# A two-layer graph kernel on one core: Gelu in place in the accumulators, the residual added from PSUM in one instruction, and the next sweep opened behind that add

## What is computed

```python
x = x + gnn0(relu(layernorm(x)), adj)   # max over the first 25 neighbours, concat, W0, bias, relu
h = relu(layernorm(x)) @ W              # layer 1: attention over the graph
e   = leaky_relu(s1[:, :, None] + s2[:, None, :], 0.4)   # s1 = h @ a1, s2 = h @ a2
att = softmax(where(adj > 0, e, -1e20), axis=1)
x = x + gelu(att @ h)
# 8 graphs (batches), N = 2048 nodes, C = 256 channels, fp32
```

## Time and profile before

| what | value |
|---|---|
| time, median of 3 runs | 4289.71 us (4282.42 to 4291.24) |
| the profiled execution: its own time | 4286.7 us |
| its span, first to last instruction | 4284.9 us |
| POOL busy | 3099.6 us (72%), 3205 instructions |
| DVE busy | 3347.2 us (78%) |
| PE busy | 2678.6 us (63%) |
| ACT busy | 1963.2 us (46%) |
| mean granted TensorE clock | 0.716 of full speed |

### The profile page before, as it was taken

One profiled execution on the slowest core, in us unless ns is written; L12 is line 12 of the kernel. 1 busy time (PEld: TensorE's weight loads), 2 busy tenths in 40 slices (PEclk: granted clock), 3 DMA queues, 4 the chain that ended last, 5 costly groups with the idle time before them and its releaser, 6 DMA issues. The chain is left out here.

```text
span 4284.9 us, 43700 instructions
## 1 busy us (share of the span) xinstructions
PE 2678.6 (63%) x13568; PEld 1997.2 (47%) x13568; DVE 3347.2 (78%) x7261; ACT 1963.2 (46%) x2364; POOL 3099.6 (72%) x3205
## 2 busy tenths in 40 slices
PE   2334446666666676566666666666666666666669
PEld 2222235444454554455444544455445445545457
DVE  5666689966898669986799768996689866998655
ACT  4222255632665236643466325553256532664146
POOL 5777777777777777777777777777777777777720
PEclk8555556777777777777777777777777767777779
DMA  6555556666666766666666666667666666666531
GB/s 211 169 158 181 175 183 215 209 221 217 204 214 208 232 214 196 216 219 227 202 217 204 224 214 214 216 198 230 209 213 219 206 220 225 193 214 203 175 109 55
DMA packets 412751, 860.10 MB, mean 201 GB/s; under 512 B 67299, under 2 KB 248422, under 8 KB 396134
## 3 DMA queue, kind: packets, MB, share of 16 engines
q0 software_dynamic: 153600, 419.64, 31.8%
q1 hardware_dynamic: 258918, 437.67, 30.2%
HBM read 714.43 MB, written 142.61 MB: 200 GB/s over the span
## 5 line engine op out<-in xcount | busy, mean ns | idle before, releaser
L411 POOL DMA_INDIRECT gb<-h_table,idx x3200 | 3098.9, 968 | 1012.2 <-issue 962.1
L980 PE MATMUL ps_av<-hz,lk 128*128 128x256 f32 x3712 | 1123.1, 469 | 118.6 <-DVE hz L817 118.6
L730 DVE TENSOR_REDUCE hl<-gb 128x256 f32<-128x3328 f32 x128 | 740.5, 5785 | 401.5 <-DMA gb<-h_table,idx 401.1
L980 PEld LDWEIGHTS ps_av<-hz,lk 128*128 128x128 f32 x3712 | 884.7, 245 | 351.9 <-issue 192.1
L730 DVE TENSOR_REDUCE gb<-gb 128x256 f32<-128x3328 f32 x128 | 748.6, 5848 | 10.5 <-DMA gb<-h_table,idx 10.5
L1035 PE MATMUL ps_l<-cf,hl 128*128 128x128 f32 x512 | 117.5, 373 | 673.9 <-issue 485.2
L1039 PE MATMUL ps_l<-w,hcat 128*128 128x256 f32 x1024 | 455.0, 622 | 86.4 <-ACT hcat L542 86.4
L542 ACT COPY hcat<-ps_l 128x512 f32<-128x512 f32 x128 | 74.9, 585 | 832.3 <-PE ps_l L1035 832.3
L428 ACT ACTIVATE sg<-ps_c 128x1024 bf16<-128x1024 bf16 x256 | 259.9, 1015 | 377.1 <-PE ps_c L956 358.3
L1035 PEld LDWEIGHTS ps_l<-cf,hl 128*128 128x128 f32 x512 | 77.1, 187 | 720.6 <-issue 720.6
L1039 PEld LDWEIGHTS ps_l<-w,hcat 128*128 128x128 f32 x1024 | 307.5, 314 | 194.3 <-ACT hcat L542 130.5
(11 more groups left out here) (130 smaller groups left out, 3634.9 us busy)
## 6 DMA issues: line engine op xcount, KB each, us to landing
ad<-in_adj SPq DMA_DIRECT2D x128, 1024.0 KB
p_rest<-lk SPq DMA_DIRECT2D x112, 512.0 KB, 3.5
lk<-p_rest SPq DMA_DIRECT2D x112, 512.0 KB, 4.1
gb<-h_table,idx POOLq DMA_INDIRECT x3200
edges_t<-stage SPq DMA_DIRECT2D x32, 1024.0 KB, 7.0
edge<-edges_t SPq DMA_DIRECT2D x64, 512.0 KB, 6.7
xl<-in_x SPq DMA_DIRECT2D x128, 128.0 KB, 5.5
hl<-h_table SPq DMA_DIRECT2D x128, 128.0 KB, 5.7
```

What stands on the lines that cost most here:

```text
L411: pool.indirect_dma_start(gb[c][:, s + (c > 0), :], None, table[tb], bass.IndirectOffsetOnAxis(idx[u][:, k:k + 1], 0)).then_inc(gathered[c ...
L730: V.tensor_reduce(dst, gb[c][:, :, :].rearrange("p k c -> p c k"), AX.X, ALU.max).then_inc(maxed[c], 1)
L980: ins = T.matmul(accumulator(k), lk_of(jj, u, drain)[:, k * P:(k + 1) * P], hz[jj][:, :], start=False, stop=False)
```

## The change

Gelu writes back into `ps_av` (no wait for `out_stored` on ACT any more). DVE adds `xo` to `ps_av` in one instruction of 2048 columns into `go`, and waits for `out_stored` itself; outside the drain that add stands ahead of the step's first reduce, in the drain where it was. `open_sweep` waits for the add (`res_ready`) in place of the Gelu. Outside the drain, in the steps t = 1 and t = 9, `open_sweep` and `av(it - 2, 0)` move from behind the product with W0 to behind the product that makes `h` (L1059 to L1062), just ahead of `av(it - 1, 1)`. This holds for round 1 too, where step 1 has an opening but no flush.

```diff
             def flush(f):
                 act.wait_ge(S["sweep_done"], f + 1)
-                act.wait_ge(S["out_stored"], f * 16)
-                nc.scalar.activation(go[:, :, :], ps_av[:, :].rearrange("p (k c) -> p k c", c=C), ACT.Gelu
-                                     ).then_inc(S["gelu_done"], 1)
+                nc.scalar.activation(ps_av[:, :], ps_av[:, :], ACT.Gelu).then_inc(S["gelu_done"], 1)
...
             def flush(o, f):
                 dve.wait_ge(S["gelu_done"], f + 1)
                 dve.wait_ge(S["xo_in"], f * 16 + 16)
+                dve.wait_ge(S["out_stored"], f * 16)
                 dve.wait_ge(order, o.n)
-                for k in range(0, 8, PIECE // C):
-                    ins = V.tensor_tensor(go[:, k:k + PIECE // C, :], go[:, k:k + PIECE // C, :],
-                                          xo[:, k:k + PIECE // C, :], ALU.add)
-                ins.then_inc(S["res_ready"], 1)
+                V.tensor_tensor(go[:, :, :], ps_av[:, :].rearrange("p (k c) -> p k c", c=C), xo[:, :, :], ALU.add
+                                ).then_inc(S["res_ready"], 1)
...
+                if fl is not None and not drain:
+                    flush(o, fl)
                 if g:
                     chunk_max(o, 0, v + 1)
-                if fl is not None:
+                if fl is not None and drain:
                     flush(o, fl)
...
             def open_sweep(f):
                 if not (f == 0):
-                    pe.wait_ge(S["gelu_done"], f)
+                    pe.wait_ge(S["res_ready"], f)
...
-                if old and t % 8 == 1:
+                if old and t % 8 == 1 and drain:
                     open_sweep(b * 2 - 2 + t // 8)
-                    if drain:
-                        open_last()
-                if old:
+                    open_last()
+                if old and (t % 8 != 1 or drain):
                     av(it - 2, 0, 1 - u, drain, whole=drain and t > 0)
                 if a:
                     transpose_signs(v + 4)
...
                     ins.then_inc(S["h_done"], 1)
+                if old and t % 8 == 1 and not drain:
+                    open_sweep(b * 2 - 2 + t // 8)
+                    av(it - 2, 0, 1 - u, drain)
                 if old and drain and t:
                     av(it - 1, 1, 1 - u, drain, whole=True, close=t == 8)
```

## The result

| | before | after |
|---|---|---|
| time, median of 6 runs | 4290.07 us (4282.42 to 4291.24) | 4332.02 us (4322.49 to 4347.05) |
| ratio, 95% interval | | 1.0104 [1.0085, 1.0124] |
| profiled execution: own time, span | 4286.7, 4284.9 us | 4333.5, 4331.7 us |
| end of POOL's last gather | 4112.4 us | 4159.3 us |
| from there to the end of the span | 172.5 us | 172.4 us |

A forecast was written before the change was run, and what follows sets the result against it. POOL's chain of 3200 gathers plus a tail was taken as the bound. The terms -3 + 9.6 + 8.4 + 2.4 = 17.4 us gave 4304 for the profiled execution, 4307 us for the median, range 4290 to 4326.

The forecast's parts named there:

- The bound, the places, the sign: POOL's gather chain sets the time; its waits for DVE grow before tiles 4 and 12; slower, chance 0.68.
- The add from PSUM: 13 flushes outside the drain: gathers beside the add are no longer stretched, 3 us gained, ends 0 and 6.
- The add ahead of the first reduce: DVE, steps 1 and 9: the first reduce moves back by at most 2.48 us, covered by slack, no cost.
- Step 1: Rounds 1 to 7: relu waits for the moved av, making reduces late; 9.6 us lost, ends 3.6 and 15.
- 1.4 + 4.3, since PE no longer pauses there: Step 1 on PE: us taken for the opening and for av, between fast (1.0, 3.72) and slow (1.88, 5.50) ends.
- Round 1 of step 1: Second reduce at 638.4, 6 us late; less 2.8 us of slack, 3.1 us reach POOL.
- Step 9: Rounds 1 to 7: load_p waits on SP, a burst follows, xn lands late; 8.4 us lost, ends -1 and 20.
- The drain: PE's opening waits for the add as well as the Gelu: 2.4 us later, not regained in the tail.
- (a): Not slower: both waits covered, step 1's av ends at L1061 + 5.6 or sooner; 4290 to 4293 us, chance 0.23.
- (b): Faster: step 1's stores go earlier, gathers land sooner, waits for DVE shrink; 4281 us at most, chance 0.04.
- (c): Much slower: the long add holds POOL's gathers despite PSUM; some 20 us over the forecast, 4325 us, chance 0.07.
- the sum of all upper ends: Upper ends of add, step 1, step 9 and drain: 0 + 15 + 20 + 2.5 = 37.5 us.

The follow-up runs named there:

- the repeat: The changed kernel itself, run again on the same chip as the run with ten unused matmuls: 4331.08 us, 1.0115 [1.01, 1.013].
- the two with one move alone: Kernel before, only the opening and av(it - 2, 0) moved, in step 1 (4299.39 us, 1.0038) or in step 9 (4313.32 us, 1.0075).

## Why the prediction was wrong, point by point

- **The bound, the places, the sign: right.** POOL's chain took all of the growth, the waits rose before tiles 4 and 12 and, but for the second chunk of tile 3 in round 1, nowhere else by more than 1.5 us, DVE's wait moved from a landing to the relu and to `xn`.
- **The add from PSUM: right.** -3 us forecast; the stretch went from 3.28 to 0.10 us, the sum of the gathers' durations fell by 2.7. The add ahead of the first reduce cost nothing, as forecast: the waits before tiles 3 and 11 rose by at most 0.3 us.
- **Step 1, 9.6 us forecast, 18.7 measured (16.4 before tile 4, 2.3 before tile 3's second chunk).** The failed term is "1.4 + 4.3, since PE no longer pauses there". There is no middle value: over the two profiles of the kernel after, the first product took either 3.7 us, the relu then starting 4.9 to 5.1 us behind the end of L1059 (9 of 14 cases, waits 0.2 to 3.6, median 1.06), or 5.3 to 6.8 us with an opening that had taken longer too, the relu starting 7.2 to 8.6 us behind (5 cases, waits 4.3 to 5.0). The middle of the sum, a relu 5.5 us behind, was met in none. The chain behind the relu was sized well: 2.0 us of relu, 2.5 of leaky, the second reduce at once behind it, and with the fast product round 2 lost 0.9 us more than before (1.07 against 0.20) where 1.2 was forecast. What was left out is that slack was gone, so that a slow product, which holds the relu back by 2.1 to 3.7 us, reaches POOL as a wait of 4.3 to 5.0 us, and that the pause had only moved: in step 9 of round 2 PE waited 1.76, 2.03, 3.17 and 1.22 us in the 14 us ahead of L1059. The argument "PE no longer pauses" looked at the wait that was removed, not at those in front of the new place. The rows gave a warning, though no more: L1061's 1.06 us for four matmuls in the earlier trace rows is the low clock's duration, 0.61 the other's, so the new place begins at the low level. They could not tell which product would follow: L1059 took 1.06 us in all 14 cases, ahead of the fast products too.
- **Round 1 of step 1.** 3.1 us forecast, 5.0 + 2.3 measured. The chain gave 638.4 for the second reduce, it began at 639.99, and late enough to hold the second chunk's gathers of tile 3 as well, which the prediction had not looked at. In the repeat round 1 met the fast product and lost 3.6 us.
- **Step 9, 8.4 us forecast, 29.4 more measured.** The order of events was right (`load_p`, burst, `xn`, L884, first reduce). This is the larger miss, and the step that failed is its sum, in which three terms were too small. `load_p` issued 6.8 us behind L1059 at the mean of rounds 1 to 6, not 5.8 (clock). The burst took 17.1 us from `load_p` to `xn`, not 15, although it moved at 353 GB/s: SP's own issue stood for 3.19 us in the middle in round 2, and for 2.7 to 5.2 over the six rounds, for which the sum had no term. In rounds 4 to 6, where I had left L1061 in its place, it came 1.3 us later against the gathers. So `x1` came 24.6 us behind the end of L1059 at the mean, 3.1 more than the 21.5 of the sum. In rounds 4 to 6 that makes 9.5 us, and the late L1059 3.9: 13.4 of the 13.8 that were missing. In rounds 1 to 3 it makes 9.0, less 2.0 by which L1059 came earlier than forecast: 7.0 of the 7.2. Each term was 15% small or so; the slack had been subtracted already, so the errors went to POOL whole, six times.
- **The drain: right in its place, but it doesn't show in this execution.** The end of the opening, counted from the end of the last `h` product, went from 22.11 to 24.42 us: 2.3 us, where the sum had 2.4, as the next lines show against the earlier trace rows. The tail did not grow in this execution, mainly since the last tile's `h` product came 1.75 us earlier behind POOL's end; that seems luck, as over all profiles the tail took 172.2 us at the mean of the four with the old drain (170.1 to 173.4) and 173.7 at that of the eight with the new one (172.0 to 175.3).

```profile
4199.48 1.86 ACT L508 ACTIVATE ps_av<-ps_av 128x2048 f32<-128x2048 f32 x1
...
4201.38 2.29 DVE L823 TENSOR_TENSOR go<-ps_av,xo 128x2048 f32<-128x2048 f32 x1 [1.54 <-ACT ps_av L508]
...
4203.73 1.88 PE L1019 MATMUL ps_av<-zeros 1*128 1x512 bf16 x4 [8.96 <-DVE go L823]
```

- **The rivals.** (a) fell: where its fast product came, in nine of 14 cases of step 1, it ended 5.9 us or more behind the start of L1059 in place of 5.6, and in step 9 the burst alone was too long. (b) fell: the waits grew. (c) did not happen, but is shown to be real by the one long add from SBUF.
- **The range.** Its top, 4326, was about the sum of all upper ends, 37.5 us over before, and both large terms went past theirs, step 1 with 18.7 against 15 and step 9 with 29.4 against 20. The bounds had varied one number at a time (the product's speed, the rate of the transfers) and had none for SP's issue standing still or for L1061 coming late.

What stays open: why the first product of step 1 sometimes finds the low clock and sometimes not, from round to round of one execution; round 2 of the kernel after had pauses of 4.09 and 2.03 us ahead of it and found the high one. How often an execution gets which does move its time. In the six profiles in which the relu of step 1 waits for the moved product, one, two, three, four, four and six of the seven products were slow, and the waits before tile 4 and tile 3's second chunk were 10.1, 15.9, 21.1, 23.8, 21.6 and 29.6 us, some 4 us for each slow product. That would fit the spread of the times, 24.6 us over the six runs of the kernel after against 8.8 for the kernel before, but the other runs have no trace, so it isn't shown. Nor is it shown why SP's issue stalls.

## What to carry to other kernels

When work is moved behind a late product, look at the rows just in front of its new place, not the old one: the durations of small matmuls there show the clock's level. Where they show the low one, carry two prices through the whole sum, the fast product's and the slow one's, and never a middle that neither has. Before putting a wait on a queue, list what it issues behind that wait and how much of it is needed soon: here issuing the waiting load last removed one delay and giving the item its own buffer the other, and with both the loss was gone. Once the slack of a bound engine is used up, an error of 3 us in a chain is multiplied by the number of rounds, so the range has to be built on the repeated term.

## What the runs showed of the hardware

- **A long DVE add with two SBUF operands holds the gather that starts inside it until it ends.** 1.07 to 2.48 us at a flush, 19.9 us over 13; with one operand in PSUM 0.10. With four short adds it is 3.28 us over 13 in the kernel before and 5.6 and 5.1 in the two with one move alone; in each of these two, one gather was held over three short adds in a row (by 2.2 and 1.5 us), so short adds are no sure protection.
- **SP's issue itself can stall.** The `load_p` that took 0.32 us to issue took 3.19 us behind a burst of 0.5 + 1 + 0.13 + 0.26 + 1 MB (up to 5.17 in the kernel after, at most 1.81 in the kernel before, 0.88 with `load_adj` ahead of the wait), and all that was queued behind it went out later by as much. SP's loads of edges (L242) already took up to 3.77 us to issue in the kernel before, so the stall could have been seen there.
- **The same 16 matmuls took 3.7 us or up to 6.8 us in one execution,** at a granted clock of 1.00 and of 0.55. In step 9 ten unused matmuls in the pause ahead moved them to the fast side in all seven rounds, where in the repeat without them all seven were slow.
